# Image attention, first stage: probability transposes moved from two to three steps behind the exponentials and next to the scores, value products moved from even to odd steps, four places for the row sums

## What is computed

```python
B, S_lat, _ = latents.shape
x = layer_norm(image_embeds, ln1_g, ln1_b)
l = layer_norm(latents, ln2_g, ln2_b)
q = l @ Wq
kv_in = jnp.concatenate([x, l], axis=1)
k, v = jnp.split(kv_in @ Wkv, 2, axis=-1)
q, k, v = (to_heads(q), to_heads(k), to_heads(v))
scale = 1.0 / np.sqrt(np.sqrt(DIM_HEAD))
w = jnp.einsum('bhqd,bhkd->bhqk', q * scale, k * scale)
w = jax.nn.softmax(w.astype(jnp.float32), axis=-1).astype(q.dtype)
out = jnp.einsum('bhqk,bhkd->bhqd', w, v)
return out.transpose(0, 2, 1, 3).reshape(B, S_lat, INNER) @ Wo
```

## Time and profile before

| | |
|---|---|
| median of 3 runs | 2053.88 us (2050.75 to 2053.91) |
| profiled execution, its own time | 2035.62 us |
| its span | 2033.8 us |
| mean granted clock of TensorE | 0.889 |
| busy over the span: PE, weight loads, DVE, ACT, POOL | 78%, 49%, 61%, 42%, 32% |
| first stage with its last sub-steps, 33 to 790 us: PE, DVE, ACT, POOL busy | 641.0, 534.8, 488.4, 462.2 of 757 us |

### The profile page before, as it was taken

The page is one execution under the profiler, slowest core; times in us unless marked ns, Lnnn a source line. Parts: engine busy times, 40 slices in busy tenths (PEclk is TensorE's granted clock), DMA queues, the critical chain, the costliest instruction groups (busy, mean ns, idle before and its releaser), DMA issues.

```text
span 2033.8 us, 31415 instructions
## 1 busy us (share of the span) xinstructions
PE 1576.4 (78%) x11325; PEld 990.8 (49%) x11325; DVE 1234.0 (61%) x2952; ACT 846.2 (42%) x1899; POOL 644.7 (32%) x770
## 2 busy tenths in 40 slices
PE   4898878977987987856249689968966886389997
PEld 2566656665665665634136435533543333324444
DVE  5777677767776674544975756644465556633433
ACT  4677656755775673521006335543212542200111
POOL 3566657756654664430002252100002101100000
PEclk9999999998999999875658889998986977699997
DMA  5111110000000001230000000000000000000000
GB/s 221 40 57 49 49 48 18 18 15 8 21 15 15 27 19 42 77 130 0 0 0 0 9 5 1 2 1 0 1 1 0 1 1 0 1 0 6 0 6 11
DMA packets 22638, 46.67 MB, mean 23 GB/s; under 512 B 4967, under 2 KB 16322, under 8 KB 21331
## 3 DMA queue, kind: packets, MB, share of 16 engines
q1 hardware_dynamic: 21015, 42.56, 6.6%
q0 software_dynamic: 1472, 2.12, 0.3%
HBM read 30.59 MB, written 12.66 MB: 21 GB/s over the span
## 4 chain that ended last, share of the span: by engine, by line
PE 48%; DVE 33%; issue 8%; ACT 7%; POOL 2%; DMA 1%; ACTq 0%; DVEq 0%; SPq 0%; POOLq 0%
PE banks L475 9%; DVE work L734 6%; PE banks L2472 3%; PE banks L1856 3%; PE banks L2468 3%; DVE work L752 3%; DVE xn L421 3%; PE banks L689 3%; DVE work L808 2%; DVE work L800 2%; PE banks L678 2%; PE banks L704 2%; ACT work L836 2%; PE banks L450 2%; PE banks L1839 2%
## 5 line engine op out<-in xcount | busy, mean ns | idle before, releaser
L954 POOL TENSOR_TENSOR work<-work 128x512 bf16<-128x512 f32 (+1 forms) x448 | 373.7, 861 | 74.7 <-ACT work L851 70.9
L836 ACT ACTIVATE work<-banks,work 128x666 f32<-128x666 f32 x256 | 208.3, 814 | 250.8 <-DVE work L734 167.4
L689 PE MATMUL banks<-const,work 128*128 128x128 f32 (+1 forms) x1536 | 229.4, 280 | 71.7 <-ACT work L851 67.8
L734 DVE TENSOR_REDUCE work<-banks 128x1 f32<-128x666 f32 x256 | 215.8, 843 | 51.5 <-PE banks L678 51.1
L415 POOL TENSOR_TENSOR norm_room<-norm_room,minus_half 128x4 f32<-128x4 f32 x48 | 50.1, 1045 | 569.2 <-DVE norm_room L410 569.2
L689 PEld LDWEIGHTS banks<-const,work 128*128 128x128 f32 (+1 forms) x1536 | 155.6, 135 | 115.1 <-ACT work L836 64.2
L678 PE MATMUL banks<-work 128*128 128x512 bf16 (+1 forms) x1024 | 189.3, 307 | 0.4 <-issue 0.4
L704 PE MATMUL banks<-work 128*64 128x256 bf16 x2304 | 158.9, 282 | 13.9 <-POOL work L954 12.8
L475 PE MATMUL banks<-work,weights_b 128*128 128x512 bf16 (+1 forms) x840 | 158.4, 347 | 11.8 <-DVE work L2180 5.3
L450 PE MATMUL banks<-const,xn 128*128 128x128 f32 x176 | 41.6, 381 | 145.3 <-DVE xn L421 89.4
L851 ACT ACTIVATE work<-banks 128x512 f32<-128x512 f32 x256 | 150.5, 588 | 2.3 <-PE banks L689 2.3
(11 more groups left out here) (386 smaller groups left out, 3139.9 us busy)
## 6 DMA issues: line engine op xcount, KB each, us to landing
work<-work SPq DMA_DIRECT2D x64, 166.5 KB, 2.7
sorted<-in_pads SPq DMA_DIRECT2D x10, 838.5 KB
weights_b<-in_weights SPq DMA_DIRECT2D x1, 4120.0 KB, 23.7
weights_b<-in_weights SPq DMA_DIRECT2D x1, 2824.0 KB, 9.7
weights_a<-in_weights SPq DMA_DIRECT2D x1, 2056.0 KB, 8.9
weights_a<-in_weights SPq DMA_DIRECT2D x1, 2050.0 KB, 10.0
work<-sorted SPq DMA_DIRECT2D x15, 129.0 KB, 2.2
rows<-in_rows SPq DMA_DIRECT2D x1, 1496.0 KB, 13.2
```

What stands on the lines that cost most here:

```text
L689: m = pe.transpose(ps[0:rows, c:c + P], prob[:, t * P:t * P + rows], self.eye)
L734: ve.tensor_reduce(self.neg_max[i % 4], self.slot[i % 2][:, 0:KEYS0], AX_X, ALU.max, negate=True).then_inc(self.mark("max"))
L836: ac.activation(self.probs[i % 4], self.slot[i % 2][:, 0:KEYS0], ACT.Exp, bias=self.neg_max[i % 4], accum_out=self.sums[u % 2][:, 2 * j + ...
L954: po.tensor_tensor(parts[:, :, :, 0], exact, parts[:, :, :, 1], ALU.subtract).then_inc(self.mark(event, i - 3))
```

## The change

The transposes of sub-step i - 3 (instead of i - 2) are issued in step i, straight behind the scores in every step. The value products, the spread transposes, the reciprocal and L746 move by one step, from even to odd steps, and stand behind the transposes. The output projections L632 move from odd to even steps, in front of a projection L475 of the same step. The copies (L851, L752, L757) and POOL's splits follow one step later. Four places for sums instead of two let the exponential of a unit's first sub-step wait for a reciprocal of four units before. The number of instructions is the same on every engine. In the changed file, L613 is line 615; other lines named here keep their numbers.

```diff
-        self.sums = [self.place(4) for _ in range(2)]
+        self.sums = [self.place(4) for _ in range(4)]
...
-        late = i - 8 * PAIRS - 7
+        late = i - 8 * PAIRS - 8
...
-        back, part = i // 4 - 2, i % 4
+        back, part = (i - 1) // 4 - 2, (i - 1) % 4
...
             if i < SUBS:
                 self.image_scores_pe(pe, i)
+            if 3 <= i < SUBS + 3:
+                self.image_turn_pe(pe, i - 3)
             back, part = self.image_back(i)
...
-            if 2 <= i < SUBS + 2:
-                self.image_turn_pe(pe, i - 2)
...
-                ve.reciprocal(self.inverse[back % 2], self.sums[back % 2]).then_inc(self.mark("inverted"))
+                ve.reciprocal(self.inverse[back % 2], self.sums[back % 4]).then_inc(self.mark("inverted"))
...
-            if 2 <= i < SUBS + 2:
-                u, _, _, _, h, j = self.image_sub(i - 2)
+            if 3 <= i < SUBS + 3:
+                u, _, _, _, h, j = self.image_sub(i - 3)
                 if u >= 2:
                     ve.wait_ge(*self.at("weighed", u - 1))
-                ve.wait_ge(*self.at("turned_b", i - 1))
+                ve.wait_ge(*self.at("turned_b", i - 2))
...
-                if i % 4 == 0 and u >= 2:
-                    ac.wait_ge(*self.at("inverted", u - 1))
+                if i % 4 == 0 and u >= 4:
+                    ac.wait_ge(*self.at("inverted", u - 3))
...
-                              accum_out=self.sums[u % 2][:, 2 * j + h:2 * j + h + 1]).then_inc(self.mark("exp"))
+                              accum_out=self.sums[u % 4][:, 2 * j + h:2 * j + h + 1]).then_inc(self.mark("exp"))
...
-            if 2 <= i < SUBS + 2:
-                u, _, _, _, h, j = self.image_sub(i - 2)
+            if 3 <= i < SUBS + 3:
+                u, _, _, _, h, j = self.image_sub(i - 3)
                 if u >= 2:
                     ac.wait_ge(*self.at("weighed", u - 1))
-                ac.wait_ge(*self.at("turned_a", i - 1))
+                ac.wait_ge(*self.at("turned_a", i - 2))
...
-            if 3 <= i < SUBS + 3:
-                u, _, _, _, h, j = self.image_sub(i - 3)
+            if 4 <= i < SUBS + 4:
+                u, _, _, _, h, j = self.image_sub(i - 4)
```

More of the change, by code:

```diff
@@ L547, in image_chores @@
                 out.append((("once", "once_scale", "again", "again_scale", "columns")[i - first], b))
-        late = i - 8 * PAIRS - 7 - 6
+        late = i - 8 * PAIRS - 8 - 6
         if late >= 0 and late % (8 * PAIRS) in (1, 2, 4) and late // (8 * PAIRS) < BATCH - 1:
@@ L568, in image_steps @@
     def image_steps(self):
-        return range(SUBS + 15)
+        return range(SUBS + 16)
     def image_sub(self, i):
@@ L746, in image_ve @@
                 ve.tensor_tensor(out, self.out_bank[:, 0:2 * P], out, ALU.mult).then_inc(self.mark("mixed"))
-            if 2 <= i < SUBS + 2:
-                u, _, _, _, h, j = self.image_sub(i - 2)
+            if 3 <= i < SUBS + 3:
+                u, _, _, _, h, j = self.image_sub(i - 3)
                 if u >= 2:
                     ve.wait_ge(*self.at("weighed", u - 1))
-                ve.wait_ge(*self.at("turned_b", i - 1))
+                ve.wait_ge(*self.at("turned_b", i - 2))
                 ve.tensor_copy(self.probs_t[u % 2][:, h, 4:KT0, j * P:(j + 1) * P],
-                               self.bank_b[:, 0:2 * P].rearrange("p (t n) -> p t n", t=2)).then_inc(self.mark("kept_b", i - 2))
+                               self.bank_b[:, 0:2 * P].rearrange("p (t n) -> p t n", t=2)).then_inc(self.mark("kept_b", i - 3))
                 if (h, j) == (0, 0):
-                    ve.wait_ge(*self.at("kept_b", i - 2))
+                    ve.wait_ge(*self.at("kept_b", i - 3))
                     parts = self.probs_parts[u % 2][:, h, 4:KT0, 0:P, :]
@@ L845, in image_ac @@
                 ac.activation(out, self.out_bank[:, 2 * P:4 * P], ACT.Copy).then_inc(self.mark("spread_kept"))
-            if 2 <= i < SUBS + 2:
-                u, _, _, _, h, j = self.image_sub(i - 2)
+            if 3 <= i < SUBS + 3:
+                u, _, _, _, h, j = self.image_sub(i - 3)
                 if u >= 2:
                     ac.wait_ge(*self.at("weighed", u - 1))
-                ac.wait_ge(*self.at("turned_a", i - 1))
+                ac.wait_ge(*self.at("turned_a", i - 2))
                 ac.activation(self.probs_t[u % 2][:, h, 0:4, j * P:(j + 1) * P],
-                              self.bank_a.rearrange("p (t n) -> p t n", t=4), ACT.Copy).then_inc(self.mark("kept_a", i - 2))
+                              self.bank_a.rearrange("p (t n) -> p t n", t=4), ACT.Copy).then_inc(self.mark("kept_a", i - 3))
             if i == 4:
@@ L942, in image_po @@
                     self.route_send_po(po, b)
-            if 3 <= i < SUBS + 3:
-                u, _, _, _, h, j = self.image_sub(i - 3)
+            if 4 <= i < SUBS + 4:
+                u, _, _, _, h, j = self.image_sub(i - 4)
                 cols = slice(j * P, (j + 1) * P)
-                po.wait_ge(*self.at("kept_a", i - 3))
+                po.wait_ge(*self.at("kept_a", i - 4))
                 for tiles, event in (((0, 4), "low_a"), ((4, KT0), "low_b")):
@@ L950, in image_po @@
                             continue
-                        po.wait_ge(*self.at("kept_b", i - 3))
+                        po.wait_ge(*self.at("kept_b", i - 4))
                     exact = self.probs_t[u % 2][:, h, tiles[0]:tiles[1], cols]
                     parts = self.probs_parts[u % 2][:, h, tiles[0]:tiles[1], cols, :]
-                    po.tensor_tensor(parts[:, :, :, 0], exact, parts[:, :, :, 1], ALU.subtract).then_inc(self.mark(event, i - 3))
+                    po.tensor_tensor(parts[:, :, :, 0], exact, parts[:, :, :, 1], ALU.subtract).then_inc(self.mark(event, i - 4))
             if i >= 32 and i % 4 == 0:
```

## The result

| | before | after |
|---|---|---|
| median | 2052.32 us (4 runs, 2046.35 to 2053.91) | 2106.63 us (4 runs, 2098.58 to 2112.05) |
| profiled execution, its own time and span | 2035.62, 2033.8 | 2098.58, 2096.8 |
| mean granted clock | 0.889 | 0.884 |

The ratio is 1.0267, with a 95% interval of 1.0225 to 1.0309: slower, by 54.3 us. The forecast was slower by 35.8, and 2106.6 lies just outside its range (2066 to 2104). The sign was right, and so was the chain of waits that costs the time; its main term was too small.

What follows compares the result with a forecast made beforehand. A circle of waits, not one engine's work, was taken to bound the kernel; 31.6 + 14.2 - 11.7 - 6.4 + 3.2 + 4.9 = +35.8 us on 2053.9 gave 2089 us, range 2066 to 2104.

Steps and rivals of the forecast that it cites:

- its main term: The 20 regular groups of eight steps, each 1.58 us longer: +31.6 us.
- The ring: Longest circle of waits over PE, ACT and DVE per unit of four steps: 11.41 us against 10.62, +0.79.
- The first rival: Steps even out, the third step removing transposes' weight-load waits for exponentials; 20.2 to 21.1 us per group, 2021.5 us; chance 0.07.
- transposes to value products 0.68: Link on PE: value products start 0.68 us after the start of transposes that waited.
- from these to ACT's copy L845 0.53: Link from PE to ACT: copy L845 starts 0.53 us after the spread transposes start.
- The nine groups at batch changes: Groups at the three batch changes, taken to be slowed like regular groups: +14.2 us.
- what gets better there: Output projections' waits for lows less new waits for the addition, -11.7 us; half of PE's waits for POOL's splits, -6.4.
- The first two groups: Opening groups of the first stage, slowed by the same circle of waits: +3.2 us.
- The last steps: Last eight steps, without projections: 11.41 us per four steps instead of 8.98, +4.9 us.
- one more step at the end: Extra step at the end, having only work that runs beside other work: 0, at most 1 us.
- the third rival: PE's longer idle times lower the granted clock, value products take 2.13 us instead of 1.21: 2108 to 2145 us; chance 0.09.
- frees nothing: Transposes reading probabilities one step older gain nothing, since they wait for the single bank 4.

Runs made afterwards that it cites:

- experiment 4: Kernel before with only the probability transposes moved straight behind the scores, still two steps behind the exponentials: 2148.05 us, ratio 1.0471 to before.
- experiment 1: Changed kernel with value products and spread transposes put back between scores and probability transposes in odd steps: 2038.79 us, ratio 0.9927 to the kernel before.
- (7): Changed kernel with L746 issued one step later on DVE, behind the maximum of the following even step: 2049.99 us, ratio 1.0006 to the kernel before.
- 8: Changed kernel with products back between scores and transposes, and L746 one step later behind the maximum: 2013.87 us, ratio 0.9833 to the kernel before.
- experiment 3: Kernel before with transposes three steps behind, four places for sums, copies and splits one step later; products in even steps before the transposes: 2057.37 us, ratio 1.0017.
- experiment 2: Kernel before with four places for the sums instead of two, nothing else: 2051.99 us, ratio 0.9988 to the kernel before.
- experiment 5: Changed kernel with the value products' semaphore waits issued in front of the transposes: 2100.87 us, ratio 1.0259 to the kernel before.
- experiment 6: Changed kernel with ACT's wait for the previous batch's output projections before L845 kept only where needed: 2097.31 us in its one run.

## Why the prediction was right, and where it was off

- **The ring.** Right, link by link, and shown from four sides: the order alone costs (experiment 4), its undoing gives more than all back (1), taking DVE's part out of the ring does as well (7), and every start in the timeline follows its predecessor of the forecast. The first rival, that the steps even out, is ruled out by its own test: L845 waited for the spread transposes in all 64 units. Where its condition holds, in experiments 1 and 8 with L845 straight behind the exponential, groups of 20.76 and 20.00 come, about the 20.2 to 21.1 it named; but the weight loads still wait 55.7 us for exponentials in experiment 1 (64.2 in before), so the third step didn't take these waits away.
- **The step that failed: "transposes to value products 0.68".** That number is from transposes followed by scores (569.76 to 570.44); followed by value products it is 0.78, and it stands twice in the ring. That is 0.20 per unit and 0.40 per group, 11.6 us on 29 groups. The other links came out within 0.03 us each, together 0.06 long. The 0.10 could have been suspected from the trace of before: products start 0.66 us behind the scores (565.00 to 565.66), transposes that don't wait 0.57 in the median.
- **The link "from these to ACT's copy L845 0.53"** was right for the later batches and 0.06 too long for the first, which has one wait less (0.47). I had taken 0.53 from the last batch without knowing why it was that long. So the ring is 11.41 + 0.20 + 0.06 = 11.67 in the later batches, a group of 23.35, and 11.61 and 23.23 in the first, +2.0 to +2.1 against +1.58. By the rule of the sum, 20 groups at the measured pace give 466.53 - 424.78 = +41.8 in place of +31.6, and nine groups at 2.09 give +18.8 in place of +14.2. These two make 14.8 of the 18.5 us that the medians' +54.3 lies over +35.8, and 11.6 of them are the products' 0.10.
- **The nine groups at batch changes.** +3.5 less the ring's 18.8 leaves -15.3 for what gets better there; the forecast had -11.7 - 6.4 = -18.1. The waits say the same: 18.9 to nothing for the lows, 7.3 of new waits for the addition (I had 7.2), 12.8 to nothing for POOL. I had taken half of the last. So some of these waits were not on the path, or the longer time at the lower clock took some of the gain back; the traces don't part the two.
- **The ends.** The first two groups (and one step) cost +0.4 and not +3.2; they take about 53 us in both kernels, where as many regular steps take 45.8 and 49.3, so something else sets their pace, and I should not have put the whole ring on them. The last steps cost +7.3 and not +4.9. From the scores of step 249 to the last scores it is +3.7 (13.18 to 16.88 us), the ring. The other +3.7 lies behind the last scores (19.45 to 23.11 us to the last output projection), where the changed kernel has four sets of transposes left and before three: the "one more step at the end" that the forecast put at 0, at most 1, is not hidden.
- **The clock.** It did not fall where the third rival had it fall: it is 1.00 in all regular stretches, though PE now stops before three of four sets of transposes, 0.89 us at the longest. So the third rival is out. Nor did stops of 1.30 us before every second set bring it down in the regular groups of experiment 4. At the batch changes and in the opening the time at 0.50 grew from 30.7 to 41.0 us, for which the forecast had nothing. The pattern that the Trainium skill warns of (TensorE: Matmul & The Clock Gate, "A second HAM failure mode: psum-queue depth-cycling") is present in the regular stretches, in the changed kernel more than before, and the trace does not show its effect there.
- **The third step itself.** The prediction says that it "frees nothing". Experiment 3 against experiment 2 shows 0.45 us per group, since L757 no longer stands between L746 and the next maximum. In the change it stands there again, because L746 moved too, so this gain is not in it.
- **What I had not seen at all:** that the odd steps protect the distance to POOL's splits. It had no term of its own in the sum, since the change moves both; experiment 3, which moves one of them, paid 21 us of waits for it.

Open: why the value products' weights are not loaded ahead of them; it is not their waits (experiment 5), and I did not try products of another width. Open too: what the longer time at the lower clock costs at the batch changes.

## What to carry to other kernels

In a software pipeline over one PSUM bank, an instruction's place inside the step can decide more than its distance in steps, as it did here: list the starts round the longest ring of waits, and put PE's independent work where the ring would wait for another engine anyway, not between the release of the bank and the next scores. Moving a consumer one step later does not help by itself if what it waits for is the bank and not the data; what it gained here (0.45 us per group, experiment 3) came from an instruction that left the ring with it. Look also at what keeps its distance to a slower engine when only one of two is moved. Take each link from a pair of instructions of the same kinds, since 0.1 us twice per unit in some 60 units is over a fifth of the effect here.

## What the runs showed of the hardware

- The time from the start of one series of matmuls to the next depends on what follows, not only on what precedes: behind 128 x 128 f32 transposes that waited, scores start after 0.68 us and the 64-wide bf16 products after 0.77 to 0.78; moving the products' semaphore waits ahead left 0.77. The first weight load of the scores starts 0.10 us ahead of its matmul, that of the products with it.
- A semaphore wait on ACT whose condition was met long before costs about 0.06 us where ACT is idle and the next wait is on the path (L845 0.53 us behind L615 with it, 0.47 to 0.48 without, both in the change and in experiment 6).
- TensorE's granted clock stays at its upper level, 1.00, in stretches where PE stops for 0.5 to 0.9 us in three of four steps of 1.7 to 3.6 us (for 1.30 in every second step of experiment 4). It was at 0.50 for 41.0 us in the opening groups and at the batch changes of the change, and for 30.7 in before.
